# Attention with heads: score places of two PSUM banks, 800-column exponentials, values mixed for two key tiles at a time

## What is computed

```python
# x: 16 batches x 100 queries x 128;  ctx: 16 x 1444 keys x 128;  H = 16 heads of 8
qh, kh, vh = (proj(q, wq, bq), proj(k, wk, bk), proj(v, wv, bv))
scores = jnp.einsum('bhqd,bhkd->bhqk', qh, kh) / np.sqrt(DK).astype(jnp.float32)
attn = jax.nn.softmax(scores, axis=-1)
out = jnp.einsum('bhqk,bhkd->bhqd', attn, vh)
out = out.transpose(0, 2, 1, 3).reshape(b, s, D)
return out @ wo + bo
```

## Time and profile before

| | us |
|---|---|
| three runs: median (lowest to highest) | 2774.57 (2773.25 to 2779.51) |
| profiled execution: its own time | 2766.48 |
| its span, first to last instruction | 2764.8 |
| busy in the span: TensorE / ScalarE / VectorE | 2223.0 / 1446.4 / 941.6 |
| exponentials L951: 768, busy / ScalarE idle before them | 859.7 / 337.1 |
| scores L886: 2304 matmuls, busy | 580.4 |
| mixes L850: 9216 records, busy | 504.7 |

### The profile page before, as it was taken

The page is one execution under the profiler, slowest core; times in us unless marked ns, Lnnn a source line. Parts: engine busy times, 40 slices in busy tenths (PEclk is TensorE's granted clock), DMA queues, the critical chain, the costliest instruction groups (busy, mean ns, idle before and its releaser), DMA issues. The chain is left out here.

```text
span 2764.8 us, 46622 instructions
## 1 busy us (share of the span) xinstructions
PE 2223.0 (80%) x18032; PEld 1466.4 (53%) x18033; DVE 941.6 (34%) x1702; ACT 1446.4 (52%) x1764; POOL 228.6 (8%) x280
## 2 busy tenths in 40 slices
PE   4767877877977918999951999996992999994998
PEld 2544743843744604666531555554771556663787
DVE  4453443454344441222153222225224122214111
ACT  2235345254344416888840778884221788882433
POOL 2113023022131200000000000000000000000000
PEclk9989989989988958999975999997995999995999
DMA  6968349269177393887715577761007487860000
GB/s 201 280 185 294 111 172 340 67 222 330 51 269 258 111 212 85 183 185 169 169 40 129 122 176 173 178 137 56 1 0 163 101 180 175 183 148 16 16 23 20
DMA packets 151689, 409.67 MB, mean 148 GB/s; under 512 B 18842, under 2 KB 65808, under 8 KB 150896
## 3 DMA queue, kind: packets, MB, share of 16 engines
q1 hardware_dynamic: 136832, 370.63, 50.2%
q0 software_dynamic: 14672, 36.45, 4.4%
HBM read 269.41 MB, written 126.71 MB: 143 GB/s over the span
## 5 line engine op out<-in xcount | busy, mean ns | idle before, releaser
L951 ACT ACTIVATE a_probs<-a_score 128x1200 f32<-128x1200 f32 x768 | 859.7, 1171 | 337.1 <-PE a_score L886 337.1
L886 PE MATMUL a_score<-a_qstack,a_kstack 128*128 128x400 f32 x2304 | 580.4, 374 | 88.0 <-issue 86.9
L886 PEld LDWEIGHTS a_score<-a_qstack,a_kstack 128*128 128x128 f32 x2304 | 380.4, 190 | 261.1 <-issue 198.8
L850 PE MATMUL a_numer<-a_probs,a_v 128*18 128x200 f32 (+1 forms) x9216 | 504.7, 337 | 10.9 <-DVEq L1065 10.3
L850 PEld LDWEIGHTS a_numer<-a_probs,a_v 128*18 128x18 f32 (+1 forms) x9216 | 213.8, 97 | 224.4 <-issue 113.9
L1023 DVE TENSOR_TENSOR a_qstack<-a_qrep,k_groupmask 128x1600 fp32r<-128x1600 f32 x48 | 87.3, 1823 | 319.2 <-PE a_score L886 272.9
L1699 ACT ACTIVATE f0r_hidden<-f0r_ph 128x512 f32<-128x512 f32 x112 | 66.9, 597 | 192.2 <-PE f0r_ph L1626 192.2
L1459 ACT ACTIVATE f3d_hidden<-f3d_ph,f_b 128x400 f32<-128x400 f32 x128 | 75.9, 593 | 116.1 <-PE f3d_ph L1417 108.5
L1638 PE MATMUL f0r_py<-f_w,f0r_hidden 128*128 x896 | 126.2, 284 | 11.8 <-issue 5.4
L1626 PE MATMUL f0r_ph<-f0r_xsT,f0r_w 128*128 (+1 forms) x896 | 123.7, 282 | 3.9 <-DVE f0r_xsT L1787 3.1
L1638 PEld LDWEIGHTS f0r_py<-f_w,f0r_hidden 128*128 128x128 f32 x896 | 108.5, 191 | 24.1 <-issue 22.5
(11 more groups left out here) (355 smaller groups left out, 2625.1 us busy)
## 6 DMA issues: line engine op xcount, KB each, us to landing
a_kstack<-keys SPq DMA_DIRECT2D x192, 722.0 KB, 11.6
keys<-kv_split SPq DMA_DIRECT2D x96, 512.0 KB
values<-kv_vst SPq DMA_DIRECT2D x32, 1296.0 KB
a_v<-values SPq DMA_DIRECT2D x48, 864.0 KB
kv_ctxT<-in_ctxT SPq DMA_DIRECT2D x32, 722.0 KB
keys<-kv_split SPq DMA_DIRECT2D x48, 420.0 KB
l0a_ctxT<-in_ctxT SPq DMA_DIRECT2D x16, 722.0 KB
l0a_ctx<-in_ctx SPq DMA_DIRECT2D x16, 704.0 KB
```

Of the source, the lines that this page charges most:

```text
L850: last = pe.matmul(numer[32 * g:32 * g + PC, p * 2 * SQ:(p + 1) * 2 * SQ], v[0:rows(t), j, t, (2 * g + p) * PC:(2 * g + p + 1) * PC], prob ...
L886: last = pe.matmul(to, kstack[:, j, g * SK + t * 128:g * SK + (t + 1) * 128], qstack[:, j, g * GH:(g + 1) * GH, :], start=True, stop=not s ...
L951: act.activation(probs[:, n % NP, :].rearrange("p (g q) -> p g q", g=SPAN), slot_ps[:, n % 2, :, 0:GQ], ACT.Exp, scale=HSCALE).then_inc(ex ...
```

## The change

All of it is in `heads_attention` and its constants. `SPAN` becomes 2 and a new constant `DEEP` = 3 gives the number of places, so the same six banks hold three slots of two units. A batch has 24 slots. Slot n of scores waits for exponential n-3. The exponential (now L954) has 800 columns, and there are `NP` = 12 buffers of them. Mixes are written down in pairs: tiles t and t+1 (t even) behind slot (4t+7)//2 + 2 = 2t+5; the last pair stands behind slot 1 of the next batch. The spread matmul moves from behind slot 4 of 16 to behind slot 5 of 24, the output projection from slot 8 to slot 9. Transfers and VectorE's work are as before.

```diff
-SPAN = 3
+SPAN = 2
+DEEP = 3
 SLOTS = UNITS // SPAN
-NP = 6
+NP = 12
...
-        score = c.ps("score", [128, 2 * SPAN * 512])
+        score = c.ps("score", [128, DEEP * SPAN * 512])
...
-                if n >= 2:
-                    pe.wait_ge(exped, n - 1)
+                if n >= DEEP:
+                    pe.wait_ge(exped, n - DEEP + 1)
                 for i in range(SPAN):
                     t, g = divmod(s * SPAN + i, GROUPS)
-                    to = slot_ps[:, n % 2, i, 0:GQ]
+                    to = slot_ps[:, n % DEEP, i, 0:GQ]
...
-                        for t in range(KT):
-                            at = (4 * t + 3) // SPAN + 2
+                        for t in range(0, KT, 2):
+                            at = (4 * t + 7) // SPAN + 2
                             if at == s and b < B:
                                 mix(b, t)
+                                mix(b, t + 1)
                             if at == s + SLOTS and b:
                                 mix(b - 1, t)
-                        if s == 4 and b:
+                                mix(b - 1, t + 1)
+                        if s == 5 and b:
...
-                        if s == 8 and b:
+                        if s == 9 and b:
...
-                act.activation(probs[:, n % NP, :].rearrange("p (g q) -> p g q", g=SPAN), slot_ps[:, n % 2, :, 0:GQ],
+                act.activation(probs[:, n % NP, :].rearrange("p (g q) -> p g q", g=SPAN), slot_ps[:, n % DEEP, :, 0:GQ],
```

More of the change, by code:

```diff
@@ L774, in heads_attention @@
             qlog = c.sb("qlog", [128, 512])
-        score = c.ps("score", [128, 2 * SPAN * 512])
+        score = c.ps("score", [128, DEEP * SPAN * 512])
         numer = c.ps("numer", [128, 512])
         misc = c.ps("misc", [128, 512])
-        slot_ps = score[:, :].rearrange("p (s g c) -> p s g c", s=2, g=SPAN)
+        slot_ps = score[:, :].rearrange("p (s g c) -> p s g c", s=DEEP, g=SPAN)
         q_full, q_free, q_ready, q_split = c.sems("q_full q_free q_ready q_split")
```

## The result

The changed kernel takes 2804.5 us in the median of 5 runs (2795.31 to 2812.08), the kernel before 2774.57 in 5 runs (2760.3 to 2779.51): slower, by a ratio of 1.0113 (95% interval 1.0076 to 1.0151). The difference is clear of no change and under 2%. The forecast was 2803.5 us, with 0.80 on slower.

What follows compares the result with a forecast made beforehand. TensorE, issuing back to back, was taken to bound the old kernel; the changed one, a chain through TensorE and ScalarE. Stages 1 and 3 add 13.7 us each, stage 2 1.5: 28.9 over 2774.57 gives 2803.5 us, range 2783 to 2835.

Steps and rivals of the forecast that it cites:

- round: One loop of eight scores and a double mix, six per batch: 3.62 us forecast, 3.14 for TensorE alone, break-even 3.47.
- The chain: Scores wait for an exponential that stands behind the double mix, through TensorE and ScalarE: 3.62 us, TensorE stalling about 0.5.
- The batch: Period in stages 1 and 3: 6 x 3.62 + 0.74 = 22.46 us, 0.91 more than 21.55.
- The gain on TensorE: Pairing mixes removes six switches per batch and shortens each second half: 0.32 us x 6 = 1.9 us per batch.
- Stage 2: Middle attention stage, held by VectorE's masking loop at 22.44 us; waiting replaced, 0.1 us per batch added, 1.5 us in all.
- Rival A: In the attention stages the loop through both engines does not close: 20.1 us a batch, 2717 us in all; chance 0.09.
- Rival B: Loop through both engines near break-even, 3.45 to 3.50 us: 2770 to 2780 us, no measurable difference; chance 0.08.
- Rival C: TensorE's clock falls to half in the new pauses of the attention: up to 82 us more, 2885 us; chance 0.06.

## Why the prediction was right, point by point

| link of a round | forecast | measured |
|---|---|---|
| exponential ends, scores begin | 0.07 | 0.05 |
| two scores and handover | 0.56 | 0.56 |
| double mix until next scores | 1.48 | 1.48 |
| two scores until their exponential | 0.67 | 0.67 |
| exponential | 0.84 | 0.84 |
| round | 3.62 | 3.60 |

- **The chain** is shown, not only argued. Lengthening one link by 0.09 us lengthened the batch by six times that. Undoing the pairs took 0.78 of the 0.94 us away at the same number of exponentials. Moving the mix by a slot did nothing, moving the keys did nothing, and more releases between exponential and reuse, with the mix further behind, turned the loss into a gain.
- **The batch** came to 22.49 us with a round of 3.60, where 6 x 3.60 + 0.74 would be 22.34. The missing part is for the most part one row:

```profile
1215.68 1.55 PE L851 MATMUL a_numer<-a_probs,a_v 128*18 128x200 f32 x32
...
1219.28 1.67 PE L851 MATMUL a_numer<-a_probs,a_v 128*18 128x200 f32 x32
```

  The mix of the last two tiles (1219.28) takes 1.67 us instead of 1.55, since the last tile has 36 rows. I had no term for it; it and the 0.02 us that I had too much in each round cancelled.
- **The gain on TensorE** (1.9 us a batch) exists. With single mixes in the same slots TensorE needs 2 x 1.73 = 3.46 us for what a double round does in 3.60 - 0.46 = 3.14 us, which is 0.32 us x 6. It was given back as waiting, and more with it: 0.46 us x 6 = 2.8.
- **Stage 2** lost 2.7 us (1.5 forecast; a batch 0.16 us, where the forecast added 0.1 that no row gives). There the chain replaced the waits for VectorE and was not added to them: the weight loads of TensorE's mixes waited for it 3.2 us in 14 batches after, 14.7 us before.

```profile
PEld a_numer L851 <- DVEq L1068: 3.2, 5, 1.2
```

- **Rival A** (a batch of 20.1 us) failed as the places of two units left no release to spare. The kernel with six places, whose chain is shorter, came near its number: 20.76 us a batch, and 20.66 with early keys.
- **Rival B** (break-even) needed a round of 3.47; it was 3.60. **Rival C** (the clock): the granted clock stayed at 1.00 from 1100 to 1400 with 0.36 us of standing in each round. The prediction's own evidence for this was weaker than it says: the twelve pauses a batch that it counts in the kernel before are switches of 0.20 us, and TensorE was busy in 346.61 of 347.20 us there.
- **The whole time** was met to 1.0 us, which is luck beyond the stages' 29.7 against 28.9: runs of one kernel spread over 17 us. The prediction took 0.2% for what a measurement can tell from no change; the interval of the ratio turned out to be 0.4% to each side. The low end of its range, 2783, is also lower than its 22.1 us a batch give (15 x 0.55 x 2 = 16.5 us, or 2791 without stage 2).

## What to carry to other kernels

Where a producer and a consumer share a few places, busy time says little. Write down the loop: release, refill, the other work that stands between two refills in the producer's queue, the first result after it, and the release that the next refill waits for. The length of this loop is a floor of its own for the period. Batching the other work (here the mixes) makes the loop longer. Here it cost 2.1 us a batch with two places and 0.8 with three, and paid with six; where the places are cut from a fixed area, smaller ones with more releases may serve better than large ones. With six places it was slow all the same (23.71) until the mix stood far enough behind its exponentials. Length and place of the wait can both be read from one round of the timeline.

## What the runs showed of the hardware beyond what was expected

- Exponentials in a row overlap by 0.11 to 0.14 us at all three sizes: 400 columns take 0.53 us and start every 0.39 ((3.28 - 0.53)/7), 800 columns 0.84 and 0.73 ((3.03 - 0.84)/3), 1200 columns 1.17 and 1.06 ((3.29 - 1.17)/2). A bias from a tile adds 0.09 us at 800 and at 1200 columns alike.
- In a double mix the change from a tile of 128 rows to one of 36 costs 0.12 us (1.67 against 1.55).
- From the end of an exponential to the weight load of scores that waits for it, it is 0.05 us in 288 of 333 such waits of the changed kernel.
- A pause alone does not say whether the clock falls. In the kernel before, 1.75 us of standing at 1563.87 were followed by a granted clock of 0.50 (1.2 GHz) from 1565.20 to 1568.60; 2.10 us of standing at 1610.66 were followed by 1.00 (2.4 GHz) from 1611.40 to 1614.80.
- The part of the program ahead of stage 1, the same instructions in every kernel here, took from 1042.8 to 1063.9 us.
